# Last layer of a fused network: narrower peak tiles, a fourth score bank, other work put between score pairs, and reordered loads, Pool steps and normalisation

## The reference

```
qkv = (x @ W_qkv + b_qkv).reshape(b, n, H, D, 3)
qkv = jnp.transpose(qkv, (4, 0, 2, 1, 3))
q, k, v = (qkv[0], qkv[1], qkv[2])
scores = jnp.einsum('bhnd,bhmd->bhnm', q, k) * scale
att = jax.nn.softmax(scores, axis=-1)
out = jnp.einsum('bhnm,bhmd->bhnd', att, v)
return out @ W_proj + b_proj
...
router_probs = jax.nn.softmax(x @ router_w + router_b, axis=-1)
top_p, top_i = jax.lax.top_k(router_probs, K)
top_p = top_p / jnp.sum(top_p, axis=-1, keepdims=True)
expert_out = jnp.einsum('bnd,edc->bnec', x, expert_w) + expert_b
gathered = jnp.take_along_axis(expert_out, top_i[..., None], axis=2)
return jnp.einsum('bnk,bnkc->bnc', top_p, gathered)
...
t = t + _L3_attn_ref(_ln_t(t), L3_attn_W_qkv, L3_attn_b_qkv, L3_attn_W_proj, L3_attn_b_proj)
t = t + _L3_ffn_ref(_ln_t(t), L3_ffn_router_w, L3_ffn_router_b, L3_ffn_expert_w, L3_ffn_expert_b)
```

## Time and profile before

| | us |
|---|---|
| median of three executions | 8477.82 |
| lowest and highest | 8460.32, 8492.71 |
| the profiled execution | 8467.15 |
| its span in the profile | 8464.8 |
| one window of the last layer in the loop | 62.5 |
| mean granted PE clock, share of full speed | 0.878 |

### The profile page before, as it was taken

The page is one execution under the profiler, slowest core; times in us unless marked ns, Lnnn a source line. Parts: engine busy times, 40 slices in busy tenths (PEclk is TensorE's granted clock), DMA queues, the critical chain, the costliest instruction groups (busy, mean ns, idle before and its releaser), DMA issues. The chain is left out here.

```text
span 8464.8 us, 152843 instructions
## 1 busy us (share of the span) xinstructions
PE 6645.8 (79%) x48081; PEld 2768.6 (33%) x48272; DVE 5057.2 (60%) x7798; ACT 5212.4 (62%) x8588; POOL 2198.2 (26%) x3329
## 2 busy tenths in 40 slices
PE   3457888888888888666648888888888888888887
PEld 3223444444444444334432222222222222222222
DVE  5544555555555555423327777777777777777775
ACT  0116777877877787500006776776767767777676
POOL 0021222222222222200012333333333333333333
PEclk7668998899999999855658999999999999999999
DMA  1010000000000000111110000000000000000000
GB/s 70 11 40 9 5 6 6 6 5 6 6 5 6 6 6 5 17 20 20 20 16 5 7 7 9 7 9 7 7 9 7 7 9 7 9 7 7 9 7 7
DMA packets 502054, 92.38 MB, mean 11 GB/s; under 512 B 475742, under 2 KB 501295, under 8 KB 501423
## 3 DMA queue, kind: packets, MB, share of 16 engines
q1 hardware_dynamic: 500399, 86.02, 5.6%
q10 hardware_dynamic: 1152, 0.05, 0.0%
HBM read 52.47 MB, written 33.56 MB: 10 GB/s over the span
## 5 line engine op out<-in xcount | busy, mean ns | idle before, releaser
L2014 DVE TENSOR_REDUCE d_peaks<-d_p_k 128x2 f32<-128x1024 f32 x2048 | 2445.8, 1220 | 825.8 <-PE d_p_k L1865 807.3
L1733 ACT ACTIVATE d_wt<-d_p_s 128x512 f32<-128x512 f32 x4096 | 2214.2, 605 | 734.9 <-PE d_p_s L1837 728.7
L735 ACT ACTIVATE b_sq<-b_p_s 128x1024 f32<-128x1024 f32 (+3 forms) x1536 | 1269.7, 827 | 371.9 <-PE b_p_s L831 364.6
L744 ACT ACTIVATE b_wt<-b_sq 128x1024 f32<-128x1024 f32 (+3 forms) x1536 | 1328.1, 865 | 222.1 <-POOL b_sq L703 222.1
L1837 PE MATMUL d_p_s<-d_qT,d_kT 64*128 64x512 bf16 x4096 | 1278.2, 390 | 215.2 <-ACT d_wt L1733 91.7
L1849 PE MATMUL d_p_o<-d_wt,d_v_pad 128*32 128x512 f32 x8192 | 1135.3, 627 | 0.7 <-ACT d_wt L1733 0.7
L831 PE MATMUL b_p_s<-b_qT,b_kT 128*128 128x512 bf16 (+3 forms) x2881 | 756.2, 362 | 223.7 <-ACT b_sq L735 207.0
L703 POOL TENSOR_SCALAR_AFFINE_SELECT b_sq<-b_sq 128x256 f32<-128x256 f32 x1024 | 422.4, 418 | 1922.3 <-ACT b_sq L735 1922.3
L1865 PE MATMUL d_p_k<-d_kT,d_qT 64*128 64x512 bf16 x4096 | 878.9, 394 | 18.6 <-DVE d_peaks L2014 16.7
L843 PE MATMUL b_p_o<-b_wt,b_v_pad 128*32 128x512 f32 (+3 forms) x6144 | 706.1, 536 | 1.2 <-ACT b_wt L744 1.2
L1837 PEld LDWEIGHTS d_p_s<-d_qT,d_kT 64*128 64x128 bf16 x4096 | 320.2, 95 | 874.6 <-ACT d_wt L1733 391.7
(11 more groups left out here) (278 smaller groups left out, 9201.4 us busy)
## 6 DMA issues: line engine op xcount, KB each, us to landing
w<-in_L_conv_W SPq DMA_DIRECT2D x64, 128.0 KB, 2.1
t<-rows SPq DMA_DIRECT2D x64, 128.0 KB, 1.8
b_x_in<-t SPq DMA_DIRECT2D x64, 128.0 KB, 2.6
t<-b_result SPq DMA_DIRECT2D x64, 128.0 KB, 2.2
c_x_in<-t SPq DMA_DIRECT2D x64, 128.0 KB, 2.7
t<-c_result SPq DMA_DIRECT2D x64, 128.0 KB, 2.7
d_x_in<-t SPq DMA_DIRECT2D x64, 128.0 KB, 3.3
d_x_keep<-t SPq DMA_DIRECT2D x64, 128.0 KB, 3.8
```

Source lines behind the costliest of these rows:

```text
L735: act.activation(sq[:, n % SQ_RING, :, 0:m], p_s[n % 2][:, :, 0:m], ACT.Square).then_inc(squared, 1)
L744: act.activation(wt[:, n % RING, :, 0:m], sq[:, n % SQ_RING, :, 0:m], ACT.Silu, scale=1.0 / D).then_inc(weighed, 1)
L1733: act.activation(wt[:, n % RING, :], tile(n)[:, :], ACT.Exp, scale=SCALE).then_inc(s_used, 1)
L2014: dve.tensor_reduce(peaks[:, m, :], tile(m)[:, :, :], X, ALU.max).then_inc(k_used, 1)
```

## The change

- `S_BANKS` goes from 3 to 4. The two double tiles of `p_k` become three single banks (`K_BANKS = 3`), so PSUM is still full with `p_o`.
- PE issues scores in pairs of heads (`scores`), then one pair of peak matmuls in two banks. It first waits until both banks of a pair are free. Each peak matmul now signals its own end, and DVE takes one maximum over 512 columns for each bank.
- Within a group the order is: scores 0 and 1, `peak(2a)`, the group's other uses of the rings, scores 2 and 3, `peak(2a+1)`, `add_up` of the group before. The tables `S_MISC` and `K_MISC` give the group of every other use. Most groups have one.
- The sums are turned and divided in halves: "o0" in the own window after its first half is ready, "o1" in the window after.
- SP issues load and keep ahead of the store, and stores the result of one image earlier (`win.image("prev") - 1`).
- POOL takes the square of the centred image first in the window, and `split` is cut into `split_first` and `split_second` with the lower `shift_parts` between them.
- Several steps of DVE stand behind other m, the end of the mixture (`scaled`) as late as m = 29. `exp_router` on ACT stands behind all four exponentials of group 12.
- The hardware loop holds six windows in place of three.

```diff
-S_BANKS, K_TILES = 3, 2
+S_BANKS, K_BANKS = 4, 3
...
+S_MISC = {3: ("xlT",), 4: ("attT",), 5: ("high",), 6: ("qkv0",), 7: ("qkv1",), 9: ("low", "xl4T"), 10: ("route",),
+          11: ("experts0", "experts1"), 12: ("experts2", "experts3"), 13: ("k0",), 14: ("k1",), 15: ("q0", "q1")}
+K_MISC = {2: ("o1",), 5: ("proj",), 10: ("o0",)}
...
             def body(win):
...
-                if "prev" in win.on:
-                    store(win.image("prev"))
                 if "own" in win.on:
                     keep(win.image("own"), win.slot("own"))
+                if win.stores:
+                    store(win.image("prev") - 1)
...
+                if "prep" in win.on:
+                    squared(q, ln_step, ln_square, centred, square)
                 if "own" in win.on:
                     shift_parts(win.image("own"), win.slot("own"), 1)
...
+                for a in range(GROUPS):
+                    if "own" in win.on:
+                        scores(H * a)
+                    if "next" in win.on:
+                        peak(2 * a)
+                    for name in misc(K_MISC, a, win.on) + misc(S_MISC, a, win.on):
+                        use_misc(name)
+                    if "own" in win.on:
+                        scores(H * a + 2)
+                    if "next" in win.on:
+                        peak(2 * a + 1)
+                    if "own" in win.on and a > 0:
+                        add_up(o, win.slot("own"), a - 1)
...
                 def peak(m):
-                    dve.tensor_reduce(peaks[:, m, :], tile(m)[:, :, :], X, ALU.max).then_inc(k_used, 1)
+                    for r in range(2):
+                        dve.tensor_reduce(peaks[:, m, r:r + 1], bank((m, r))[:, :], X, ALU.max).then_inc(k_used, 1)
...
+                    if "prev" in win.on and a == 12:
+                        exp_router()
```

More of the change, by code:

```diff
@@ L1373, in k_order @@
     out = []
-    for m in range(PAIRS):
-        if "next" in on:
-            out.append(m)
-        if m in K_AFTER and "prev" in on:
-            out.append(K_AFTER[m])
+    for a in range(GROUPS):
+        out += [(2 * a, 0), (2 * a, 1)] if "next" in on else []
+        out += misc(K_MISC, a, on)
+        out += [(2 * a + 1, 0), (2 * a + 1, 1)] if "next" in on else []
     return out
@@ L1831, in seat, with scores @@
                     return p_s[win.s[name][1]]
-                def score(n):
+                def scores(n):
                     qc, kb, h = UNITS[n]
-                    rows = slice(64 * (h % 2), 64 * (h % 2) + 64)
-                    bank = seat(n)
-                    pe.matmul(bank[:, :], kT[rows, win.u, h // 2, kb * P:(kb + 1) * P],
-                              qT[rows, win.u, h // 2, qc * HALF:(qc + 1) * HALF], start=True, stop=True).then_inc(s_made, 1)
+                    wait(pe, s_used, win.s_done(n + 1) - S_BANKS)
+                    for r in range(2):
+                        rows = slice(64 * r, 64 * r + 64)
+                        pe.matmul(seat(n + r)[:, :], kT[rows, win.slot("own"), h // 2, kb * P:(kb + 1) * P],
+                                  qT[rows, win.slot("own"), h // 2, qc * HALF:(qc + 1) * HALF],
+                                  start=True, stop=True).then_inc(s_made, 1)
                 def add_up(i, slot, a):
@@ L1934, in experts @@
                 def experts(a):
+                    wait(pe, s_used, win.s_done(f"experts{2 * a + 1}") - S_BANKS)
                     banks = [seat(f"experts{2 * a + b}") for b in range(2)]
@@ L1941, in experts, with use_misc @@
                                   start=False, stop=True, skip_group_check=True).then_inc(s_made, 1)
-                for n in range(EXPS):
-                    if "own" in win.on:
-                        score(n)
-                        if n >= LAG + H - 1 and (n - LAG) % H == H - 1:
-                            add_up(o, win.u, (n - LAG) // H)
-                    if "prev" in win.on and n == LAG - 1:
+                def use_misc(name):
+                    if name == "xlT":
+                        arrived(xl_made, q + 1)
+                        turn(name, xl)
+                    elif name == "attT":
+                        arrived(k_used, win.k_done("o1"))
+                        turn(name, att)
+                    elif name == "xl4T":
+                        arrived(xl4_made, p + 1)
+                        turn(name, xl4)
+                    elif name == "high":
+                        turn_shifted(name, o, win.slot("own"), 1)
+                    elif name == "low":
+                        turn_shifted(name, nx, win.slot("next"), 0)
+                    elif name in ("qkv0", "qkv1"):
+                        project_qkv(int(name[-1]))
+                    elif name == "route":
+                        route()
+                    elif name in ("k0", "k1"):
+                        turn_parts(name, 1, int(name[-1]))
+                    elif name in ("q0", "q1"):
+                        turn_parts(name, 0, int(name[-1]))
+                    elif name in ("experts0", "experts2"):
+                        experts(int(name[-1]) // 2)
+                    elif name == "o0":
+                        turn_o(o, 0)
+                    elif name == "o1":
+                        turn_o(p, 1)
+                    elif name == "proj":
+                        project()
@@ new lines, in body @@
+                for a in range(GROUPS):
+                    if "own" in win.on:
+                        scores(H * a)
[9 more added lines that the diff above has]
+                        add_up(o, win.slot("own"), a - 1)
+                    if "prev" in win.on and a == 0:
@@ L1971, in body @@
[L1971 to L1982 removed]
+                        add_up(p, win.slot("prev"), GROUPS - 1)
```

304 lines of the change are left out of this document (139 added, 165 removed).

## The result

| | before | after |
|---|---|---|
| median of four executions, us | 8477.61 | 8403.77 |
| lowest and highest, us | 8460.32, 8492.71 | 8398.61, 8411.8 |
| the profiled execution, us | 8467.15 | 8411.8 |
| its span, us | 8464.8 | 8410.0 |
| one window in the loop, us | 62.5 | 61.6 |

The ratio of after to before is 0.9914, with a 95% interval of 0.9894 to 0.9935. The change made the kernel about 74 us faster, where I had forecast 160. The sign is right. The time lies 4 us above my own range of 8230 to 8400 us and inside the range of 8 in 10, and less than half of the gain came. The clock went down, and the window gained 0.9 us in place of 2.2.

A forecast was written before the change was run, and what follows sets the result against it. A ring of short waits, no engine full. DVE 48.3 plus 3.4, three waits 7.0, clock 1.2 and loop 0.4 make a 60.3 us window; 8467.15 - 134 - 15 = 8318 us, own range 8230 to 8400, 8 in 10: 8120 to 8465.

The forecast's parts named there:

- the ends: Outside the 61 full windows: window 63 7 us less, windows 0 and 62 some 8 us together.
- Load ahead of store: Window start: DVE's 2.9 us wait for `x_in` goes, with PE's standstill and the slow clock behind it.
- Maxima of one bank: DVE: a 512-wide maximum costs 0.61 us, so 64 cost 39.0 us where 32 wide ones cost 36.5.
- rival of halves without overlap: DVE's 512-wide maxima do not overlap, 5.1 us more DVE work, period 63.3, 8501 us; chance 0.07.
- Plain groups, three single banks: Groups with nothing else in them take 2.7 us, no shorter than 2.61; DVE's waits total 3.4 us a window.
- Wait (3): Group 12: DVE waits 2.0 us for the router's exponential, which stands behind experts and four exponentials on ACT.
- Wait (2): "low" in group 9: PE waits 2.4 us for POOL's lower `shift_parts`, and DVE loses 2.6.
- Wait (1): Early in the window, at m = 2: DVE waits 2.4 us for POOL's `square`, behind the late mixture and `combine`.
- Clock: One slow PE stretch, behind the wait for `square`: 1.2 us a window; 0 if it holds, 3.6 if it falls thrice.
- Loop: PE's "issue" gap of 2.4 us per turn: with six windows a turn 0.4 us a window, 0.8 before.
- nothing gained: Rival: the three new waits take back all the load gives, period 62.5, 8452 us; chance 0.07.
- rival in which the waits were partly hidden: Slower work elsewhere shortens the wait for `square` and the clock may hold: period 57.5, 8147 us; chance 0.22.

The follow-up runs named there:

- e5: Kernel before with only SP's load and keep issued ahead of the store, which stores one image earlier: 8218.04 us, ratio 0.9699 to before.
- e6: e3 without the wait for both peak banks ahead of a pair, each matmul waiting for its own bank: 8027.74 us, ratio 0.9470 to before.
- e7: e3 with the router's last steps earlier on DVE, so the mixture ends at m = 27, not 29: 7937.91 us, ratio 0.9361 to before.
- e1: Changed kernel with the router's exponential issued one group earlier on ACT (group 11): 8221.41 us, ratio 0.9706 to before.
- e4: Changed kernel with three windows per hardware loop turn in place of six: 8401.65 us, ratio 0.9926 to before.
- e3: Changed kernel with the router's exponential one group earlier and the lower `shift_parts` ahead of `split_first`: 7998.60 us, ratio 0.9452 to before.
- e8: Changed kernel without POOL's three adding steps of `combine`, so the result holds one expert's part only: 8283.64 us, ratio 0.9765 to before.

## Why the prediction was half right

I go by its own steps. The forecast of a window was 60.3 us, and 61.6 came. The forecast of the ends was 15 us less; the profiled spans differ by 54.8 us and the 61 windows account for 0.87 x 61 = 53, so the ends gave some 2. For window 63 there is a measure, from the start of the last peak matmul to that of the last sum's: 8428.5 - 8380.3 = 48.2 us before and 8373.5 - 8329.9 = 43.6 after, 4.6 less where 7 was forecast. Why the start of the layer and window 62 brought nothing stays open.

- **Load ahead of store.** Right on the wait: that for `x_in` is gone, and PE's standstill of 2.66 us with it. The slow clock at the start of the window went in e5, but in the whole change it stayed in most windows (see the clock below). The prediction gave no price for this edit alone, since its sum is a new walk through the window; e5 shows 4.1 us.
- **Maxima of one bank.** Right: 0.605 us from start to start and 685 ns each, forecast 0.61 and 686. The rival of halves without overlap falls. The formula in the Trainium skill ("VectorE: DVE Perf Modes", on the TRN2 errata) would make one of 512 columns 658 ns; the trace shows 685 for it alone and 605 behind another, so neither number is the formula's.
- **DVE's work.** Right: 49.2 us less 1.1 for the stretched centring is 48.1, and 48.3 was forecast.
- **Plain groups, three single banks.** Nearly right: 2.78, just outside the 2.6 to 2.75 that I gave. The wait for both banks is worth 0.08 us of it (e6); what the pairing of the scores does to it wasn't tested by itself. With "low" taken out, 7.7 - 2.73 - 1.21 = 3.8 us of waits for peaks are left, against 3.4. In e7, where nothing else covers them, they are 236.4 / 46 = 5.1 us. But the whole new order, with one other use per group, is worth more than this step said: without the three waits its window is 54.0 (e7), where the old order with the early load has 58.4 (e5). Which of its parts brings that I didn't separate.
- **Wait (3), the exponential.** This is the step that failed most, 2.96 us against 2.0, and in part by arithmetic: 0.4 + 1.5 + 4 x 0.5 is 3.9, not the 3.3 that the text has, and with 3.9 the wait would have been 2.7. Counted from the start of group 12, DVE went on with the exponential at 4.9 us (6298.54 - 6293.65) and had been there at 1.9, where I had 3.3 and 1.2. In the trace PE begins group 12 at 6293.65, its experts matmuls end at 6296.28 after a wait for a bank, ACT can copy them only then, and the exponential begins at 6298.23.
- **Wait (2), "low".** Right at 2.6 against 2.4, and DVE's loss of 2.73 against 2.6.
- **Wait (1), the square.** The wait itself was 0.92 and not 2.4. In its place the centring ahead of it was 1.1 us longer on average than before, since `combine` ran beside it. Both come from the late mixture, together 2.0. The prediction counted how long `combine` lasts but not what it does to DVE while it runs.
- **Clock.** One slow stretch was forecast, behind wait (1). In most windows it is there, and two more come behind (2) and (3), for which the prediction had a price of 3.6 us and took 1.2. The two at (1) and (3) cost little: in the window at 5075 DVE waits 0.28 us for the peaks behind the slow sum, and e1 gave hardly more than the wait. Behind that at (2) DVE waits 1.21 us. So 1.2 was the right size, but by luck: it was meant for another place. The prediction looked for waits of PE of some 2.5 us, as in the earlier trace rows. The runs give no such bound: a slow sum followed waits of 2.60 and 2.18, but also of 1.72 (at 5077.94), and not one of 1.61 (at 6254.82).
- **Loop.** Wrong: longer turns gave nothing that can be measured (e4), because the wait for the square covered the gap.

So the three waits were the right ones and the sizes were not, and what `combine` does to the centring was missing: waits for peaks 7.7 against 7.2 (3.4, 2.6 and 1.2), exponential 3.0 against 2.0, square and centring 2.0 against 2.4, DVE's work 48.1 against 48.3, and 0.8 us in gaps that no wait explains, for which the forecast had nothing. The 0.4 for the loop has no term of its own: DVE meets the turn as a wait for peaks, inside the 7.7. Together that is 1.3 us a window, 79 us, and the ends another 13. What I could have seen is that the exponential's sum was misadded, and that the forecast gain was a small difference of large terms: 62.5 - 51.7 = 10.8 us of relief against 8.6 of new waits, clock and loop. A miss of 15% in the second is more than half of the gain.

Of the rivals, "nothing gained" (8452 us) came nearer in kind than its chance of 0.07 said: the new waits took back most of what the load gave. The rival in which the waits were partly hidden falls: (2) and (3) were there at full length and their gains add up (e3), and most of what wait (1) fell short of, the centring took.

What stays open: what brings the 4.4 us between e5 and e7, what tips the clock behind the centring, in e6 above all, and which resource will set the plain group if DVE and ACT are both relieved. A fourth bank for the peaks wasn't tried.

## What to carry to other kernels

Before an operation is moved in such a ring, work out for the engine that issues it what stands ahead of it and when that is ready, and add up the chain in full; the three edits here (one condition, two calls that change places, the last steps of the mixture moved forward by one or two m) were worth 61.6 - 54.0 = 7.6 us a window. When a change has one edit that removes a wait and many that move work, try the one alone first: here it brought 3.0% where the whole brought 0.9%. After one ring is relieved, look at the next before moving more: with the peaks first, PE's wait for ACT grew and with it the group. And don't judge a stretch by one window: the one that I read first was one of the 15 of 48 without a slow sum behind its centring.

## What the runs showed of the hardware

A DVE operation with two inputs in SBUF was held by an operation of POOL that was already running. The centring began at 6252.42 and ended at 6254.09. POOL's three adding steps began at 6251.45, and their kinds apart are (groups of instructions, 5000 to 8000 us: busy, mean ns | idle before):

```profile
L1703 POOL TENSOR_TENSOR d_answers<-d_answers 128x1024 f32<-128x1024 f32 x49 | 115.5, 2357 | 3.8
L1703 POOL TENSOR_TENSOR d_answers<-d_answers 128x512 f32<-128x512 f32 x49 | 64.7, 1321 | 3.8
```

The first one thus ended at 6253.81, and the centring 0.28 us later, where it would have ended at 6252.85 by its usual duration. In e7 it is the same 0.28 us: the additions end at 6263.27 and the centring, begun at 6262.93, at 6263.55. A reduction with one input just before it, also beside POOL, lasted its usual time:

```profile
6251.97 0.41 DVE L2046 TENSOR_REDUCE d_total<-d_x_in 128x8 f32<-128x256 f32 x1
```

Without the additions (e8) the centring took 0.43 us. The Trainium skill ("SBUF — State Buffer", section "Who interferes with whom") says that a DVE instruction with two SBUF inputs and a GpSimd instruction that reads SBUF shut each other out of a shared port, for the whole instruction, in the order of issue, and that DVE's reductions don't take part. The trace agrees where it can: the operation of POOL had begun first, the centring ended only behind it, and the reduction was not held. It doesn't show the port, nor POOL held by DVE. The price was 1.3 us in the median and 1.36 at most (1.785 - 0.425), for an operation of 0.43.
